# Masked score group kept in PSUM for its maximum, head maximum turned later, and the last head's sums and weight loads moved

## The reference, cut to what matters

```
x = x + xattn(layernorm(x), ctx, ...)   # 16 query heads of 128, 4 key/value heads,
                                        # 4096 context keys + 256 own keys (causal), softmax, @ wo
x = x + mamba(layernorm(x), ...)        # in-projection (z | x, B, C | dt), conv of 4 taps, state scan of
                                        # 2 chunks of 128, gate with silu(z), rms norm, out-projection
x = x + moe(layernorm(x), ...)          # 32 experts of 192, top 6, and a shared one of 384
```

## Time and profile before

| | us |
|---|---|
| runs (three) | 1029.86, 1031.19, 1032.27; median 1031.19 |
| profiled execution, its own time | 1030.32 |
| its span | 1028.3 |
| mean granted PE clock | 0.995 of full |
| busy: PE, DVE, ACT, POOL | 986.7, 788.0, 586.2, 517.4 |

### The profile page before, as it was taken

One profiled execution on the slowest core, in us unless ns is written; L12 is line 12 of the kernel. 1 busy time (PEld: TensorE's weight loads), 2 busy tenths in 40 slices (PEclk: granted clock), 3 DMA queues, 4 the chain that ended last, 5 costly groups with the idle time before them and its releaser, 6 DMA issues.

```text
span 1028.3 us, 15218 instructions
## 1 busy us (share of the span) xinstructions
PE 986.7 (96%) x5597; PEld 856.8 (83%) x5597; DVE 788.0 (77%) x1168; ACT 586.2 (57%) x962; POOL 517.4 (50%) x481
## 2 busy tenths in 40 slices
PE   8999999998899999999999999989799999999998
PEld 7888888888888888888888888877587988888887
DVE  6645666547988888888988888889479978777775
ACT  5444434345665666656666656655279576666664
POOL 4543344330777778787777787779201032222222
PEclk9999999999999999999999999989999999999999
DMA  7647564377005020221105030040540486555540
GB/s 281 195 145 224 195 205 133 114 256 239 2 8 167 22 67 1 83 92 42 47 1 171 5 89 4 2 185 1 205 164 2 155 316 216 190 192 189 194 157 20
DMA packets 52488, 127.89 MB, mean 124 GB/s; under 512 B 3872, under 2 KB 32960, under 8 KB 50880
## 3 DMA queue, kind: packets, MB, share of 16 engines
q1 hardware_dynamic: 52416, 126.94, 36.3%
HBM read 99.64 MB, written 27.30 MB: 123 GB/s over the span
## 4 chain that ended last, share of the span: by engine, by line
PE 76%; DVE 17%; issue 3%; POOL 2%; DMA 1%; ACT 0%; DVEq 0%; SPq 0%; POOLq 0%
PE bank L523 17%; PE bank L627 13%; PE bank L505 13%; PE bank L597 12%; PE bank L905 9%; DVE run_max L1065 5%; PE bank L907 5%; DVE run_max L1055 4%; DVE weights L1085 3%; POOL run_sum L1864 2%; PE bank L713 1%; PE bank L532 1%; DVE run_max L1062 1%; DMA w_xa<-in_w_in 1%; DVE weights L1052 1%
## 5 line engine op out<-in xcount | busy, mean ns | idle before, releaser
L1864 POOL TENSOR_TENSOR run_sum<-run_sum,weights 128x512 f32<-128x512 f32 x224 | 292.9, 1307 | 52.2 <-ACT weights L1581 32.7
L627 PE MATMUL bank<-weights,vN 128*128 128x256 f32 (+1 forms) x1088 | 316.2, 378 | 0.0
L597 PE MATMUL bank<-qT_hi,kT 128*128 128x256 f32 (+1 forms) x1088 | 300.9, 360 | 2.1 <-ACT weights L1577 1.2
L597 PEld LDWEIGHTS bank<-qT_hi,kT 128*128 128x128 f32 x1088 | 198.4, 189 | 25.9 <-issue 2.4
L1577 ACT COPY weights<-bank 128x512 f32<-128x512 f32 x256 | 148.8, 585 | 123.0 <-PE bank L597 114.0
L1065 DVE TENSOR_TENSOR run_max<-bank,run_max 128x512 f32<-128x512 f32 x200 | 137.2, 686 | 55.8 <-ACT weights L1577 55.4
L627 PEld LDWEIGHTS bank<-weights,vN 128*128 128x128 f32 x1088 | 173.0, 190 | 4.2
L1581 ACT ACTIVATE weights<-weights 128x1024 f32<-128x1024 f32 x144 | 144.0, 1001 | 54.8 <-DVE weights L1085 54.8
L1085 DVE TENSOR_TENSOR weights<-weights,bank 128x1024 f32<-128x1024 f32 x128 | 154.8, 1210 | 3.2 <-PE bank L655 3.2
L597 PE MATMUL bank<-qT_lo,kT 128*128 128x256 f32 (+1 forms) x544 | 153.4, 282 | 0.0
L523 PE MATMUL bank<-w_ctx_hi,ctx_hl 128*128 128x512 f32 x512 | 144.5, 393 | 1.5 <-ACT w_ctx_hi L1543 1.3
(11 more groups left out here) (236 smaller groups left out, 1514.3 us busy)
## 6 DMA issues: line engine op xcount, KB each, us to landing
e_raw<-in_experts SPq DMA_DIRECT2D x51, 768.0 KB, 4.4
k_spill<-k_stage SPq DMA_DIRECT2D x16, 1024.0 KB, 5.3
kT<-k_spill SPq DMA_DIRECT2D x15, 1024.0 KB, 5.2
v_spill<-v_stage SPq DMA_DIRECT2D x16, 512.0 KB, 6.4
vN<-v_spill SPq DMA_DIRECT2D x16, 512.0 KB, 3.6
ctx_raw<-in_ctx SPq DMA_DIRECT2D x15, 512.0 KB, 4.1
w_raw<-in_w_qkv SPq DMA_DIRECT2D x6, 1024.0 KB, 5.1
wo_sb<-in_wo SPq DMA_DIRECT2D x4, 1024.0 KB, 7.8
```

The lines of the kernel that those rows point to most:

```text
L597: done = e.matmul(dst, kT[:, w, kt * P:(kt + 1) * P], qT[a][:, h, q0:L], start=m == 0, stop=m == 2)
L627: done = e.matmul(dst[:, q0:L], vN[:, kt, :].bitcast(F32), weights[:, cols], start=kt == 0, stop=kt == KTILES - 1)
L1864: e.tensor_tensor(run_sum[:, :], run_sum[:, :], here, ALU.add).then_inc(summed, 1)
```

## The change

1. **The masked group.** DVE adds the mask in place in PSUM, and takes the two maxima from PSUM. ACT then copies SELF to SBUF as it does the others, once DVE has done all three. A bank is now always given back by ACT's copy.
2. **The maximum later.** The fold stands in the step of the last group, behind its running maximum, and is a reduction (one operand) instead of a maximum of two halves. The turn goes from k = 2 to 4 (6 for head 0), the reduction from 3 to 5 (7), the spreading from 5 to 6 (8). Subtraction goes from 6 to 5 steps ahead and now stands before the running maximum in its step; exponentials go from 4 to 3. The sums' matmul goes one step later, `finish_head` too, on DVE (1 to 2), ACT (2 to 3); on POOL it stays behind the same sum.
3. **The last head's sums.** POOL adds groups 0 to 3 and folds them; DVE adds groups 4 to 16 in a tile of its own and folds them; two matmuls of ones add both folds in PSUM.
4. **Loads.** `run_sum` moves, so `w_xa` lies beside the values and is loaded, with `w_xb` and the small tensors, before the last head. The output weights are loaded in five parts after groups 3, 7, 11, 15 and 16 of the last head, and are split and multiplied in an order that follows (`WO_ORDER`), four steps earlier.
5. **Low parts.** DVE makes two of the five low parts of `w_xb` and `w_xa` behind the first layer norm, and three behind the second, instead of all before both.
6. The branches for groups with split weights, which no group took (`SPLIT = {}`), are removed.

```diff
-SUB_AHEAD, EXP_AHEAD, SPLIT_AHEAD = 6, 4, 2
+SUB_AHEAD, EXP_AHEAD, FINISH_LAG = 5, 3, 2
+TURN_AT, REDUCE_AT, SPREAD_AT = (6, 4), (7, 5), (8, 6)
-WO_HEADS = 4
-WO_STEP, WO_PRODUCTS = 250, 253
+OWN_SUMS = 4
+WO_STEP, WO_PRODUCTS = 246, 249
+WO_LOADS = (((0, 2), (9, 10)), ((2, 4), (10, 12)), ((4, 6), (12, 14)), ((6, 8), (14, 16)), ((8, 9),))
+WO_ORDER = (0, 1, 9, 2, 3, 10, 11, 4, 5, 12, 13, 6, 7, 14, 8, 15)
...
@@ wait_score_bank @@
-            if g == SELF:
-                port.wait_ge(maxed, plan.masked[h])
-            elif s % NG and s >= LEAD:
+            port.wait_ge(taken, s + 1)
+            if s % NG and s >= LEAD:
                 port.wait_ge(maxed, plan.maxed[s])
-            else:
-                port.wait_ge(taken, plan.taken[s])
...
@@ running_max, SELF (DVE) @@
-                    e.tensor_tensor(slot[:, g, 0:L + P], src[:, 0:L + P], causal[:, :], ALU.add).then_inc(maxed, 1)
+                    e.tensor_tensor(here[:, 0:L + P], here[:, 0:L + P], causal[:, :], ALU.add).then_inc(maxed, 1)
                     for k, (to, lo, n) in enumerate(((0, 0, L), (P, L, P))):
-                        e.tensor_tensor(run_max[:, to:to + n], run_max[:, to:to + n], slot[:, g, lo:lo + n], ALU.max).then_inc(maxed, 1)
+                        e.tensor_tensor(run_max[:, to:to + n], here[:, lo:lo + n], run_max[:, to:to + n], ALU.max).then_inc(maxed, 1)
...
@@ fold_max (DVE) @@
-                e.tensor_tensor(both_max[:, :], run_max[:, 0:L], run_max[:, L:2 * L], ALU.max).then_inc(maxed, 1)
+                e.tensor_reduce(out=both_max[:, :], in_=run_max[:, :].rearrange("p (t q) -> p q t", t=2), axis=AX, op=ALU.max).then_inc(maxed, 1)
...
@@ the loop (DVE) @@
-                running_max(s)
-                if k == 0 and h in range(NH):
-                    fold_max(h)
                 for h, j in quads_at(n + SUB_AHEAD):
                     subtract_max(h, j)
+                running_max(s)
+                if s % NG == NG - 1 and s < NH * NG:
+                    fold_max(s // NG)
+                if n - 1 in range(NG * H15 + OWN_SUMS + 1, NH * NG):
+                    add_own_weights(n - 1)
...
+            add_own_weights(NH * NG - 1)
             finish_head(H15)
...
-            for n in range(len(PAIRS)):
-                dve.wait_ge(wx_hi_done, n + 1)
-                e.tensor_tensor(pair_weights(n, 1), pair_weights(n, None), pair_weights(n, 0), ALU.subtract).then_inc(wx_lo_done, 1)
-            for tt in range(TT):
+            for tt, pairs in enumerate(((0, 1), (2, 3, 4))):
                 dve.wait_ge(wo_done, tt + 1)
                 e.tensor_tensor(x_sb[:, tt, :], x_sb[:, tt, :], bank[tt][:, :], ALU.add).then_inc(x1, 1)
                 dve.wait_ge(x1, tt + 1)
                 layernorm(2 + tt, tt, un)
+                for n in pairs:
+                    dve.wait_ge(wx_hi_done, n + 1)
+                    e.tensor_tensor(pair_weights(n, 1), pair_weights(n, None), pair_weights(n, 0), ALU.subtract).then_inc(wx_lo_done, 1)
...
@@ take_scores (ACT) @@
+                if g == SELF:
+                    act.wait_ge(maxed, plan.maxed[s])
+                else:
+                    act.wait_ge(scored, s + 1)
...
@@ sp_program @@
+                if s == NG * H15:
+                    load_later()
+                if h == H15 and (g % 4 == 3 or g == SELF):
+                    sp.wait_ge(scored, s + 1)
+                    for lo, hi in WO_LOADS[g // 4]:
+                        e.dma_start(wo_sb[:, lo:hi, :], t["wo"][:, lo:hi]).then_inc(wo_in[g // 4] if g < SELF else w_xb_in, 16)
...
             sp.wait_ge(pv, NH * NG)
             sp.wait_ge(sum_all, NH)
-            e.dma_start(w_xa[:, :, :], t["w_in"][:, :, DI:2 * DI]).then_inc(w_xa_in, 16)
             e.dma_start(w_z[:, :, :], t["w_in"][:, :, 0:DI]).then_inc(w_z_in, 16)
```

More of the change, by code:

```diff
@@ L110, in __init__ @@
                 self.groups.append((h, g))
-        self.taken, self.maxed, self.masked, self.folded = [], [], [], []
-        taken = maxed = 0
+        self.maxed = []
         for s, (h, g) in enumerate(self.groups):
-            taken += g != SELF
-            if g == SELF:
[L116 to L133, removed]
+            before = [g2 for _, g2 in self.groups[NG * h:s + 1]]
+            self.maxed.append(MAXES * h + len(before) - 1 + (2 if SELF in before else 0))
 def width(g):
@@ L242, in build_program @@
         k_stage = [back.take(f"k_stage{i}", [NKV, 2, BATCH], F32R) for i in range(2)]
-        v_stage = [back.take(f"v_stage{i}", [NKV, 2, BT, HD], F32R) for i in range(2)]
+        v_stage = [back.take(f"v_stage{i}", [NKV, BT, HD]) for i in range(2)]
         qreg = region["q"]
@@ L259, in build_program @@
         sp_ = region["spare"]
-        pT = [reg.take(f"pT{i}", [2, GW], F32R) for i, reg in enumerate([region["pt"]] * 3 + [sp_])]
         run_max = sp_.take("run_max", [GW])
+        run_sum = sp_.take("run_sum", [GW])
+        pt_ = region["pt"].again()
+        own_sum = pt_.take("own_sum", [GW])
+        own_both = pt_.take("own_both", [L])
         both_max = sp_.take("both_max", [L])
@@ L276, in build_program @@
         un = Region(nc, m23.base + 14464, 4096).take("un", [TT, DM])
-        w_in = region["v"].again()
-        w_z = w_in.take("w_z", [KD, DI])
-        w_xa = w_in.take("w_xa", [KD, DI])
+        w_z = region["v"].again().take("w_z", [KD, DI])
+        w_xa_at = Region(nc, region["v"].base + 4 * KD * DI + 2048, 4 * KD * DI)
+        w_xa = w_xa_at.take("w_xa", [KD, DI])
         x_pad = m23.take("x_pad", [NCT, PAD + L])
@@ L1082, in subtract_max @@
                 if j < NQUAD - 1:
-                    dve.wait_ge(taken, max(plan.taken[plan.number[h, 2 * j + i]] for i in range(2)))
+                    dve.wait_ge(taken, max(plan.number[h, 2 * j + i] for i in range(2)) + 1)
                     rows = quad(h, j).rearrange("p g (t q) -> p (g t) q", t=2)
@@ L1086, in subtract_max @@
                     return
-                dve.wait_ge(maxed, plan.masked[h])
+                dve.wait_ge(taken, plan.number[h, SELF] + 1)
                 rows = quad(h, j)
@@ L1139, in dve_program @@
                 h, k = divmod(s - NG, NG)
-                if k == 3 and h in range(NH):
+                if k == REDUCE_AT[h > 0] and h in range(NH):
                     reduce_rows(h)
@@ L1611, in act_program @@
                 h, k = divmod(n - NG, NG)
-                if k == 2 and h in range(H15):
+                if k == FINISH_LAG + 1 and h in range(H15):
                     finish_head(h)
```

256 lines of the change are left out of this document (105 added, 151 removed).

## The result

The changed kernel takes **999.36 us** (median of 4 runs, 998.27 to 999.48) against 1031.48 us for the kernel before in the same comparison (4 runs, 1029.86 to 1032.27): ratio 0.9688, 95% interval 0.9671 to 0.9705. The forecast was 1003, with a range of 995 to 1014. The profiled execution took 999.34 us by its own time, 30.98 less than that of before (1030.32); its span is 997.8 against 1028.3.

The account below looks back on a forecast made before the run. The prediction took the head's period to be set by PE (busy 96%) plus what DVE makes it wait for. Start +1.8, heads -23.5 and tail -5.9 gave -27.6 from 1030.3, so 1003 us, range 995 to 1014.

Parts of the forecast that it names:

- Start, +1.8: Start of the attention, head 0: spreading waits for the reduction until 260.15, first values at 262.9 instead of 261.10; 1.8 us lost.
- Heads, -23.5: Heads 1 to 14: waits at turn and spreading go, each head gains 1.83 less 0.15 of stall; 23.5 us saved.
- the last maxima 1.0 later: Last head: `finish_head` stands one step nearer to the mask, so DVE's masked-group maxima start 1.0 us later relative to PE.
- The spreading: Spreading at k = 6: DVE done at T + 13.05, PE there at T + 13.35, T being scoring of group 15; no wait.
- The stall of 0.15 behind ACT: Each head, values at k = 3: ACT's masked-group copy waits for DVE's maxima and delays quad 4's exponential; 0.15 us stall.
- Last head on DVE, 42.5: Last head: DVE's queue from the masked-group maxima through its own additions adds up to 42.5 us, against 44.6 before.
- From the sum to the projection, 15.5: Tail, PE from last sum to next projection: 13.5 us left, plus 2 charged for some 4 us at half clock.
- dt, +0.3: Tail, after the projection: DVE's step chain of dt comes about 1.3 us later; 0.3 us charged.
- the tail: After the heads: moved sums -1.1, sum to projection -5.1, dt +0.3; together 5.9 us saved.
- the masked group becomes the wait: Rival, 9 in 100: ACT waits for DVE and quad 4's values for ACT; about 1 us lost per head, 1016 us.
- The tail that gives nothing back: Rival, 9 in 100: DVE's low parts and additions block with POOL's longer, PE's clock stays low; 1010 us.
- The slower kernel: Rival, 3 in 100: maxima and fold stay at 1.3 us each, heads 2.3 us longer than forecast, tail 2; 1037 us.

Follow-up runs that it names:

- experiment 3: Kernel before the change, with POOL's additions of groups 2 to 15 narrowed to 8 of their 512 columns: 1000.9 us.
- Experiment 4: Changed kernel with extra 256-column DVE copies behind the mask in heads 2 to 14: 1008.23 us with two copies (0.88 us), 1038.17 us with five (2.26 us).
- Experiment 6: Changed kernel with all sums of the last head on POOL again: 1003.85 us.
- experiment 7: Changed kernel with five extra matmuls before the last own sum: 998.05 us; with head 0's turn, reduction, spreading at k = 4, 5, 6: 998.45; both: 998.14.
- experiment 1: Changed kernel with the masked group in SBUF again, both maxima reading SBUF and no ACT copy of it: 1004.65 us.
- experiment 2: Changed kernel with turn, reduction, spreading, subtraction, exponentials and finish_head at their old places, the new fold kept: 1003.62 us.
- experiment 5: Changed kernel with `w_xa` loaded behind the sums again: 999.97 us; all five low parts before the layer norms again: 999.7; both: 1005.93.

## Why the prediction was right, and where it was off

The direction and the size held; the kernel came out 3.6 us lower than forecast, within the range and the forecast's own range. By its steps, from the profiled executions (30.98 less in place of 27.6 less):

- **Start, +1.8.** The first values came 1.1 later, at 262.23, but the stage before had ended 0.4 earlier. From the first score matmuls (235.31 before, 234.94 after) it is 1.5 more. The mechanism is the one described: the spreading waited for the reduction, 1.82 where 260.15 - 257.8 = 2.35 was forecast. The forecast's last three terms add up to 262.55 from 260.15, not to 262.9; the trace has 262.23 - 259.39 = 2.84 from the spreading to the first values, against the 2.4 of the terms, so some 0.4 was missing from the list though the result had it.
- **Heads, -23.5, with the last maxima 1.0 later: -22.5.** Measured, from the first values to the last head's maxima: 680.83 - 261.10 = 419.7 before, 659.66 - 262.23 = 397.4 after, so -22.3. The period is 27.67 (forecast 27.5 to 27.8), the maxima 0.75 (forecast 0.75), the fold 0.71 with 0.62 to the next start (0.65). The 62 cycles that the Trainium skill gives a PSUM source ("VectorE: DVE Perf Modes", the section on the TRN2 errata) do not appear: the same two maxima take 291/358/426 ns (shortest, median, longest) from PSUM here and 291/358/425 from SBUF in experiment 3. The mask itself, the third of the operations charged there, read PSUM in the kernel before as well (547 ns, now 557).
- **The spreading.** The forecast had DVE done at T + 13.05 and PE there at T + 13.35, "close, but holds". It doesn't quite: the spreading is held by the last subtraction in every head and costs 0.37 instead of 0.21. A steady head so gains 29.25 - 27.67 = 1.58 in place of 1.68. The sum came out right because head 1 gained more: its turn had waited 1.89 in the kernel before, not 0.76.
- **The stall of 0.15 behind ACT.** At k = 3 one half group lasts 386.60 - 385.72 = 0.88 instead of 0.79, so 0.1. Experiment 4 confirms that this is where the room ends.
- **Last head on DVE, 42.5.** It took 700.92 - 659.66 = 41.3. Added up by starts, the low parts of the output weights took 15.0 instead of 15.7 and the eleven additions 7.8 instead of 8. The forecast compared its 42.5 with the 44.6 of before and took off 1.0 for the later maxima, which left 1.1; with 41.3 it is 3.3, less the same 1.0, so 2.3. Experiment 6 gives 4.5 for the same edit in the kernel as it is now, since POOL there needs 1.35 for each addition.
- **From the sum to the projection, 15.5.** It took 14.3. The clock did fall, as forecast, but the idle time before it was 2.44 and not 4, so only some 3 us ran at 0.53, or 1.4 in place of 2; experiment 7 puts it at 1.1. Where the clock stayed full the distance is 13.2, so the 13.5 beside it was 0.3 too much. That the clock fell at all in this execution was a matter of luck: the same wait left it at 1.00 in three of eight traces.
- **dt, +0.3.** The distance from the projection to the pairs is 724.32 - 715.32 = 9.0, as before: nothing.

Sum of the deviations: -0.3 at the start, -0.4 from the stage before, +0.2 in the heads, -1.2 on DVE, -1.2 behind the sum, -0.3 at dt, so -3.2 of the 3.4. The term that was mis-sized most is the tail: -5.9 with the maxima's 1.0 in the heads is 6.9 from those maxima on, and it measured 9.5.

The reasoning behind the heads was incomplete in one point. It gave the gain to the removal of both waits by both edits, and did not say that either edit alone brings three quarters of it (experiments 1 and 2). It also left out that ACT's copies behind the masked group hold DVE for 0.59 in each head. In experiment 2 this wait stands in front of the last subtraction, and the spreading waits 0.46 for that. No run undoes the loading of the output weights in five parts or their new order by itself, so what these bring is not shown.

**The rivals.** That the masked group becomes the wait is real as a mechanism, and nearer than the "1 us slower" which the forecast asked for: 0.88 more on DVE gave 1008.2, with PE waiting at k = 3. The tail that gives nothing back is refuted; the DVE operations blocked less than assumed. Its price was too low by its own rows: 27 operations at 1.15 are 31.05, which is 7.4 more than 15.7 + 8, not 3 to 5. The slower kernel was forecast at 1037 for a chain longer by some 2.3 us in each head, and experiment 4 has 1038.2 for 2.26. The two agree partly by chance: from 999.4 it was 13 heads at 2.2, and 12 us of low clock that the forecast of this rival did not have.

## What to carry to other kernels

When an operation on DVE takes twice its usual time in some places only, look at what POOL does in those windows and at how many of the operands lie in SBUF; here moving one operand to PSUM, or taking POOL's work away, restored the time. Two edits that shorten the same wait don't add: undo each alone before the credit is shared out. A long wait that hangs on a conjunction (late data and its consumer at the head of the queue) mostly goes with either half, so try the cheaper one first and look where the late data shows up next (experiment 5: 1.95 behind ACT).

## What was not expected of the hardware

- The two maxima with both operands in SBUF took 0.75, 1.85 or 2.66 us, in this order: without POOL's additions or with them narrowed (experiment 3), with them in experiment 1, and with them in the earlier trace rows and in head 1 of experiment 1 (2.75). Why 1.85 in one place and 2.66 in the other was not tried.
- Two waits of PE of 0.90 and 0.82 us with 1.44 us between their ends were followed by a clock near half for some 4 us in eight of 13 heads of one execution, and by 1.00 in the other five (experiment 4), while 0.61 alone in each head left it at 1.00. What comes after a wait isn't the same each time at other places either: five of eight after 2.44 (experiment 7), and of two executions with the same wait of PE in head 0 (2.05 before 250.00 in the kernel after, 2.06 before 249.68 with head 0's places moved), the first kept 1.00 and the second had this window:

```profile
252.00:254.00 2.00, 2.00 (x11) 2.00 (x11) 1.76 (x4) 0.75 (x2) 0.00 (x0) 0.50 1.02 419
```

Why the one falls and the other not stays open. It cost nothing in head 0, since the spreading waits for DVE anyway (0.20 in place of 1.64).
- Seven additions on DVE that each wait for the one before took 5.25 us, their starts 0.77 apart; behind one of the same shape (690.29) the next instruction, which did not wait for it, started 0.60 later.
